# Expert slots of a product-key layer: weights from the exponentials of candidate sums, and 32 slots a head instead of 27

## The reference

```python
s0 = jnp.einsum('bshq,eq->bshe', _l2norm(q0), _l2norm(keys0))
s1 = jnp.einsum('bshq,eq->bshe', _l2norm(q1), _l2norm(keys1))
sc0, ix0 = jax.lax.top_k(s0, K)          # K = 16 of 64
sc1, ix1 = jax.lax.top_k(s1, K)
cs = (sc0[..., :, None] + sc1[..., None, :]).reshape(b, s, H, K * K)
ci = (ix0[..., :, None] + ix1[..., None, :]).reshape(b, s, H, K * K)
fs, pos = jax.lax.top_k(cs, K)           # 16 of the 256 pair sums
fi = jnp.take_along_axis(ci, pos, axis=-1)
w = jax.nn.softmax(fs, axis=-1)
inner = jnp.einsum('bsd,bshkd->bshk', hidden_states, expert_down[fi])
out = jnp.einsum('bshk,bshko->bso', gelu(inner) * w, expert_up[fi])
```

## Time and profile before

| | us |
|---|---|
| median of 3 runs | 446.78 (444.7 to 447.22) |
| span of the profiled execution, first to last instruction | 440.9 |
| mean granted TensorE clock | 0.714 of full speed |
| busy: TensorE, VectorE, ScalarE, GpSimd | 306.9, 350.6, 143.5, 190.4 |

### The profile page before, as it was taken

How to read it: one execution, slowest core, us unless ns; L and a number is a source line. 1 busy time by engine, 2 the same in 40 slices (tenths; PEclk the granted TensorE clock), 3 DMA queues, 4 the chain that set the end, 5 groups by cost and what they waited for, 6 DMA issues and landing times.

```text
span 440.9 us, 7832 instructions
## 1 busy us (share of the span) xinstructions
PE 306.9 (70%) x2271; PEld 224.6 (51%) x2271; DVE 350.6 (80%) x2183; ACT 143.5 (33%) x326; POOL 190.4 (43%) x391
## 2 busy tenths in 40 slices
PE   3168456784519587999795969998676569940496
PEld 1035234453307344698663547985443259820394
DVE  1957329238999998779999979999997799997941
ACT  2126231654414266451132464224040351021300
POOL 6319932326945384469352742203064302059000
PEclk9999567898655669586587886556668866585556
DMA  6000000000000000000000000000000000000000
GB/s 226 0 0 1 1 1 0 1 0 1 1 2 0 1 2 1 2 1 2 1 0 2 1 13 0 4 0 4 1 1 13 0 1 2 2 1 12 2 1 12
DMA packets 1634, 3.50 MB, mean 8 GB/s; under 512 B 180, under 2 KB 1205, under 8 KB 1592
## 3 DMA queue, kind: packets, MB, share of 16 engines
q1 hardware_dynamic: 1592, 3.01, 1.9%
HBM read 2.49 MB, written 0.52 MB: 7 GB/s over the span
## 4 chain that ended last, share of the span: by engine, by line
DVE 42%; PE 32%; ACT 11%; POOL 10%; issue 4%; DVEq 0%; ACTq 0%; POOLq 0%
PE bank L870 8%; PE bank L536 4%; DVE Sx L1356 4%; DVE i L1362 4%; DVE i L1363 4%; DVE segmax L1237 3%; DVE vraw L1359 3%; DVE vraw L1353 2%; ACT PT L1034 2%; POOL weights L1655 2%; PE bank L674 2%; PE bank L546 2%; PE bank L732 2%; POOL slots L1670 2%; PE bank L882 2%
## 5 line engine op out<-in xcount | busy, mean ns | idle before, releaser
L870 PE MATMUL bank<-weights,onehot 108*128 108x16 f16 x1024 | 68.6, 216 | 5.3 <-DVE onehot L493 5.3
L870 PEld LDWEIGHTS bank<-weights,onehot 108*128 108x128 f16 x1024 | 68.6, 174 | 6.5 <-DVE onehot L493 5.8
L1637 POOL TENSOR_TENSOR inv<-nrm,mhalf 128x16 f32<-128x16 f32 x8 | 23.4, 2923 | 40.4 <-DVE nrm L1369 40.4
L454 POOL TENSOR_TENSOR taps<-qpad,wa 128x128 f32<-128x128 f32 x96 | 36.1, 435 | 7.8 <-ACT qpad L923 7.7
L1550 POOL TENSOR_TENSOR rstd<-veps,mhalf 128x2 f32<-128x2 f32 x16 | 11.6, 726 | 41.0 <-DVE veps L1159 40.7
L1363 DVE FIND_INDEX8 i<-vraw,Sx 128x8 uint16<-128x64 f32 x128 | 28.1, 220 | 0.0
L1362 DVE FIND_INDEX8 i<-vraw,S 128x8 uint16<-128x64 f32 x128 | 28.1, 220 | 0.0
L536 PE MATMUL bank<-wa,hat 128*128 128x128 f32 x24 | 6.9, 382 | 30.0 <-ACT hat L908 29.9
L799 PE MATMUL bank<-KB,qsT 128*128 128x256 f32 x64 | 25.5, 568 | 0.9 <-ACT qsT L1066 0.9
L1356 DVE MATCH_REPLACE8 Sx<-vraw,S 128x64 f32<-128x64 f32 x128 | 25.2, 209 | 0.0
L1412 DVE MATCH_REPLACE8 cands<-c,cands 128x54 f32<-128x54 f32 x128 | 23.7, 199 | 0.0
(11 more groups left out here) (226 smaller groups left out, 785.1 us busy)
## 6 DMA issues: line engine op xcount, KB each, us to landing
wa<-wa_dram SPq DMA_DIRECT2D x1, 747.5 KB, 4.7
wb<-wb_dram SPq DMA_DIRECT2D x1, 707.0 KB, 5.4
x_sb<-x_dram SPq DMA_DIRECT2D x4, 128.0 KB, 3.8
out_dram<-eT SPq DMA_DIRECT2D x4, 128.0 KB, 1.7
onehot<-ws_dram SPq DMA_DIRECT2D x1, 448.0 KB, 6.0
bq_row<-rows_dram SPq DMA_DIRECT2D x1, 0.5 KB
onehot<-rows_dram SPq DMA_DIRECT2D x1, 13.5 KB
```

The source lines that it names most:

```text
L454: ins = eng.tensor_tensor(tv[:, :, :, ky, kx:kx + n], q, dw[:, ky, kx:kx + n].unsqueeze(1).unsqueeze(1).broadcast_to([P, G8, G8, n]), ALU. ...
L870: last = mm(o[:, g * 16:g * 16 + 16], OHv[:, c * NT + t, g], Rv[:, c, t, g, s], start=(c == 0 and s == 0), stop=(c == NCH - 1 and s == 1))
```

## The change

- Cell weights: ScalarE takes the exponential straight from the 54 candidate sums of a head (432 elements a partition and half) into `we`. The largest value is no longer subtracted: a sum of two cosines is at most 2, and the softmax divides it out. GpSimd's subtraction and its five products go; of `cells` the five expert sums stay. VectorE signals `cand_ready` behind its sums and waits for `exp_ready` before `chosen`. The marked candidates get a buffer of their own (`candm`), since the sums have to live until ScalarE has read them.
- Slots: there are 32 a head. The cells are numbered so that 32 of them can stay in place, and the other 22 are added to slots by four sums in place, in `wem`. The copies go. The slots fill 4 x 32 = 128 partitions, so all tiles and matmuls over slots have 128 rows.
- The weights are scaled from `wem` into `wn` as before, over 32 slots. The experts are copied out of `wem` by ScalarE into a new tile `es` (one instruction a half, in steps N2r and N2s of its list), and TensorE's slot transposes wait for it (`es_ready`) as well as for `wn`.
- ScalarE's N2p waits for TensorE's scatter of the image before, not for VectorE's read of its result.

```diff
-SLOT_SUMS = [
-    (1, 1, 1, 53, -1, 8),
...
-SLOT_COPIES = [(0, 0, 1, 1), (24, 17, 9, 2), (26, 32, 1, 1)]
-SLOTS = 27
+SLOT_SUMS = [(1, 8, 53, -1), (9, 4, 43, -3), (18, 4, 44, -3), (13, 2, 32, 4)]
+SLOTS = 32
...
-        A3a.2 F8c.1 A3b.2 A1b.2 N2q.0 A3c.2 F10a.1 F10b.1 F11t.1 A4.2 F11b.1 N3a.0 F5b.2 F12.1 F5c.2 N0a.1 N4.0
+        A3a.2 F8c.1 A3b.2 A1b.2 N2q.0 A3c.2 F10a.1 F10b.1 F11t.1 A4.2 F11b.1 N2r.0 N2s.0 N3a.0 F5b.2 F12.1 F5c.2 N0a.1 N4.0
...
-        candm = cand
+        candm = sb("candm", [NT * H, CELLS])
...
-        slots = sb("slots", [2, NT * H, SLOTS])
+        es = sb("es", [NT * H, SLOTS])
...
                 pe.wait_ge(slots_ready, NT * b + halves[-1] + 1)
-                for kind, src in (("w", wn[:, :, :]), ("e", slots[:, 1, :, :])):
+                pe.wait_ge(es_ready, NT * b + halves[-1] + 1)
+                for kind, src in (("w", wn[:, :, :]), ("e", es[:, :, :])):
...
-                ac.wait_ge(dv_ready, NT * b + t + 1)
-                fn(ab[:, h, :, :], dv[:, h, :, :], ACT.Exp).then_inc(ab_ready, 1)
+
+                ac.wait_ge(cand_ready, NT * b + t + 1)
+                fn(we[:, 0, h, :], cand[:, h, :], ACT.Exp).then_inc(exp_ready, 1)
...
             def N2p(b):
                 if b >= 1:
-                    read_out(ac, "G1", b - 1)
+                    full(ac, "G1", b - 1)
...
+            def expert_slots(b, t):
+                h = slice(t * H, t * H + H)
+                if b >= 1:
+                    full(ac, "eT", b - 1)
+                ac.wait_ge(merged_ready, NT * b + t + 1)
+                fn(es[:, h, :], wem[:, 1, h, 0:SLOTS], ACT.Copy).then_inc(es_ready, 1)
...
-                link(last)
+                last.then_inc(cand_ready, 1)
+                dve.wait_ge(cand_ready, NT * b + t + 1)
...
+                dve.wait_ge(exp_ready, NT * b + t + 1)
                 dve.wait_ge(we_ready, NT * b + t + 1)
...
-                src, dst = wem[:, :, h, :], slots[:, :, h, :]
-                for at, c, step, n in SLOT_COPIES:
-                    g_.tensor_copy(dst[:, :, :, at:at + n], src[:, :, :, c:c + step * (n - 1) + 1:step])
-                for at, c, step, c2, step2, n in SLOT_SUMS:
-                    end = c2 + step2 * (n - 1) - 1
-                    last = g_.tensor_tensor(dst[:, :, :, at:at + n], src[:, :, :, c:c + n],
-                                            src[:, :, :, c2:end:step2], ALU.add)
-                link(last)
-                g_.tensor_tensor(wn[:, h, :], slots[:, 0, h, :],
+                for at, n, c, step in SLOT_SUMS:
+                    end = c + step * (n - 1) + (1 if step > 0 else -1)
+                    last = g_.tensor_tensor(wem[:, :, h, at:at + n], wem[:, :, h, at:at + n],
+                                            wem[:, :, h, c:end:step], ALU.add)
+                last.then_inc(merged_ready, 1)
+                pool.wait_ge(merged_ready, NT * b + t + 1)
+                g_.tensor_tensor(wn[:, h, :], wem[:, 0, h, 0:SLOTS],
```

43 lines of the change are left out of this document (18 added, 25 removed).

## The result

The changed kernel takes **442.08 us** in the median (439.24 to 443.43, 12 runs), the kernel before, run beside it, 446.26 us (442.84 to 450.35, 12 runs). The ratio is **0.9926, with a 95% interval of 0.9899 to 0.9954**: 0.7% faster, some 3.3 us. (The two medians lie 4.2 us apart, since the times of each kernel come in steps of about 2 us; the ratio is the better measure.) The prediction was 445.0 us, with a range of 442.0 to 448.4. By the prediction's own bound of 0.5% the kernel is faster.

What follows compares the result with a forecast made beforehand. VectorE was taken as the bound, busy 350.6 of 440.9 us. Terms -0.42 -0.28 -0.42 +1.69 -0.42 -1.95 = -1.80 us gave 439.1, plus 5.9 around the span 445.0 us; range 442.0 to 448.4, the forecast's own 443.6 to 446.6.

Steps and rivals of the forecast that it cites:

- the prediction's own bound of 0.5%: Whole kernel: 0.5% (2.2 us) taken as the measurement's own width; faster means below 444.55 us.
- The time around the span: Whole kernel: 5.9 us around the profiled span of 440.9, from the runs' median of 446.78, added to 439.1.
- The sums: VectorE's candidate sums: 0.42 us gained each at 134, 244 and 328 us, 0.42 lost at the last image.
- Merges and `kBD`, image 0: Image 0: shorter merge lets `kBD` start with `khT`; 0.7 us gained, of which 0.42 is counted in the sums.
- The clock at 174 us: Rival: image 2's stretch at 174 us gets the upper clock, 4.4 us less, 440.6 us; chance 0.10.
- the stretch: TensorE from `fT` to the first-attention outputs (L631): 9.64 us in image 2, 5.2 us in image 3 before the change.
- The wait for `es`, image 1: Image 1: `es` copies stand behind sixteen exponentials on ScalarE, so VectorE waits longer for eT; 1.69 us lost.
- The other rival, the clock against the change: Stretch behind image 1's slot transposes (from 261 us) falls to the lower clock: 4.4 us more, 449.4 us; chance 0.10.
- Image 2: Image 2's merge: TensorE reaches the transposes at 340.38 anyway, out of its fillers; nothing gained, nothing lost.
- The tail: Image 3: merge and eT come before VectorE is free, so its wait of 2.37 us goes; 1.95 us gained.
- The rival that had this gain eaten: Last image: cells hold VectorE or eT is late, so the 1.95 us is gone; 446.9 us, chance 0.12.
- the one on rows: Rival: 128 instead of 108 rows cost 3.2 us in the tail's scatter; 448.2 us, chance 0.05.

Runs made afterwards that it cites:

- the second profile of after: The changed kernel, unchanged, run once more beside the kernel before: ratio 0.9921 to before, median 441.59 us.
- esg: The changed kernel with the es copies moved from ScalarE to GpSimd, behind wn of each half: ratio 0.9933 to the kernel before, median 442.14 us.
- hold: The changed kernel, only that GpSimd's cells wait for the candidate sums of their half: ratio 0.9913 to the kernel before, median 441.37 us.
- weights_only: The kernel before with only the changed weights (exponential of the sums, expert cells only); 27 slots merged as before: ratio 0.9945 to before, 443.31 us.
- merges_only: The changed kernel with weights made as before (subtraction, exponential of 256 elements, products), so only the slots changed: ratio 0.9922 to before, 441.66 us.
- the second profile of before: The kernel before, unchanged, profiled a second time (444.5 us); against itself its ratio is 0.9991, median 446.29 us.

## Why the prediction came out as it did

**The time around the span.** The prediction added 5.9 us to the profiled span, from a median of runs and one execution. In every run whose span and time are both known the difference is about 1.8 us (446.35 and 444.5; 443.43 and 441.6). The other 4.1 us are, all but 0.5, that one execution's quicker start (3.6). For the forecast it made no difference: a sum on top of a median is right whatever the profile's luck. But the profile before was not the median execution, and comparing it with a profile of after would have shown a change of 0.7 us for the worse.

**The sums.** Right at image 0's first half: 0.88 us. The cells beside image 0's second half made it 1.52, where 1.30 was kept. In image 1 it was 0.88 in the second profile of after and 1.66 in the first. There VectorE had come 0.95 us late to the segment maxima, by the lower clock at 224 us, and the cells fell on the sums: so the 0.42 was gained in one execution and 0.36 lost in the other. In image 2 it was 1.23 and 0.88, 0.07 and 0.42 gained: the prediction had no overlap there, though by its own numbers `if_` (329.29) came before the end of the sums (329.4). In the last image 0.22 and 0.33 were lost where 0.42 was taken. What was missed: at 142 us the gain is 0.79 and 0.61 in the two profiles and not 0.42. 0.20 of it is there because the products that GpSimd no longer makes ran beside other VectorE work too. `centBD` behind the searches, a product of two operands, goes from 0.49 to 0.29 us:

```profile
139.26 0.49 DVE L1216 TENSOR_TENSOR centBD<-cent,wb 128x128 f32<-128x128 f32 x1
```

```profile
142.82 0.29 DVE L1223 TENSOR_TENSOR centBD<-cent,wb 128x128 f32<-128x128 f32 x1
```

**Merges and `kBD`, image 0.** Forecast 0.42 + 0.28 = 0.70 us; the table has 0.82 and 0.92 at negM. The merges take 1.32 + 0.62 us with a gap of 0.08, together 2.0 where 1.96 was worked out. `kBD` starts as soon as `khT` is there:

```profile
167.13 1.05 POOL L1612 TENSOR_TENSOR kBD<-khT,wa 128x512 f32<-128x512 f32 x1 [1.63 <-ACT khT L950]
```

**The clock at 174 us.** It was a rival with a chance of 0.10 and a gain of 4.4 us. It is what happened: fully, at 1.00, in five of the eleven profiles that have any part of the change, and for the larger part of the stretch, at 0.76, in the other six. The step that failed is the one that read the level in one profile as given. The price failed as well: 4.4 us was TensorE's saving (4.2 as measured), and VectorE gets 2.4 or less, because `xln` on GpSimd is late next.

**The wait for `es`, image 1.** Forecast 1.69 us lost. From 246.1 to 260.1 after loses 1.44 and 1.56, the wait itself goes from 1.13 to 2.76 and 2.68: mechanism, place and size are right. (The working has 259.05 for a sum of 259.09, and nothing hangs on it.) The sum was right to count it, and yet it was not worth its removal: esg took 2.07 us off the wait and ended where after did. The other rival, the clock against the change, came true in the experiments, in the stretch that it named: from 260 to 274 esg loses 2.75 us, hold 1.68 and weights_only 1.67; seven of the twelve profiles of the changed and the edited kernels have the stretch at 0.6 to 0.7. But it was not more idle time ahead that brought it: in esg TensorE waited 2.08 and 1.67 us there, in the two profiles of after 4.78 and 3.88, and these had 2.4 GHz.

**Image 2.** Forecast 0 for the merge; measured 0.93 and 1.41 us less of waiting for eT. This is the term of the sum that was mis-sized. It was argued that TensorE gets to the slot transposes out of its fillers anyway. In before that is so, but at 1.2 GHz: the two fillers ahead take 1.06 us. In all profiles of merges_only, weights_only and after they take 0.59 to 0.65, and then it matters that `wn` had come only 0.12 us before (340.26 against 340.38). With the short merge it is there in time; with the long one, in weights_only, TensorE waits for it:

```profile
341.88 1.10 PE L534 MATMUL bank<-wa,wn 128*108 128x128 f32 x4 [0.45 <-POOL wn L1668]
```

The transposes follow the clock too. In merges_only (the rows below) and the second profile of after both groups take 0.60 us instead of 1.06; in the first profile of after they take 0.88 and 1.06, and the gain is the smaller 0.93. So the term needs the shorter merge and the upper clock together, and the prediction took neither as a gain here.

```profile
340.71 0.60 PE L530 MATMUL bank<-wa,wn 128*128 128x128 f32 x4
341.14 0.60 PE L530 MATMUL bank<-wa,es 128*128 128x128 f32 x4
```

**The tail.** Forecast 2.37 us of wait gone, less 0.42 for the sums: 1.95. From 357 us on (-1.29 and -2.52, between two columns of the table) to the second eT at 415 (-3.24 and -4.37) the two profiles of after gain 1.95 and 1.85. The wait is gone as said and the sums lose 0.22 and 0.33; what nothing in the prediction had are 0.38 us lost between the first and the second eT. VectorE's products for `R` now run beside the second merge and take 2.14 us instead of 1.70.

```profile
409.58 2.14 DVE L1482 TENSOR_TENSOR weights<-W,cands 128x256 f16<-128x256 f16 x8
```

The rival that had this gain eaten is excluded, and so is the one on rows.

**Together**: leave out the stretch (2.42) and the late maxima behind it (0.96), and the steps of the sum come to 3.42 - 2.42 + 0.96 = 1.96 us in the profile of after, against a forecast of 1.80. That it is so close is luck: image 2's eT gave 0.9 us more than forecast, and the sums took 0.8 more in image 1 and 0.35 in image 2. In the second profile of after the same reckoning (0.97 for the stretch, nothing lost at the maxima) leaves 3.8. So the forecast was right in direction, in the wait for `es` and in the tail; it was too small by image 2 and by the clock, whose better level it held to be improbable. How much of the 3.3 us is the clock's stays open: what it gives at 174 us it partly takes at 224, and in no run was it held at one level.

## What to carry to other kernels

Compare two profiles only from a point behind which they differ by the change alone: set both to zero at the last place that the change can't have touched. One execution's luck of the clock (3.6 us here) is otherwise larger than the effect.

A wait that two edits remove is gained once, and a gain in mid-kernel is only worth what is left of it at the end: the twelve profiles of the changed and the edited kernels all came to 246 us between 1.7 and 3.7 us early, and all but one left 274 us with 1.03 us or less. The gain that reached the end in each of the eleven that have any part of the change is that of the last image.

Where a second engine's small operations fall beside those of the bounding one, it is worth trying one wait to keep them apart: hold took 0.64 us off one group of sums by an added wait on an idle engine, and the searches behind did not suffer. A gain of the whole kernel by it is not shown.

## What the runs showed of the hardware

The same kernel has more than one time. The matmuls at 42.15 us take 1.94 us in one execution of the kernel before and 3.60 in the other, and with what follows up to 78 us the total differs by 3.6 us. The runs of the unchanged kernel show this as steps, near 442.7, 444.7 and 446.4 us, and those of after near 439.3, 441.3 and 443.2. In ten of the fourteen profiles the record of the clock covers this place, and it tells the two starts apart. Below are 17 matmuls at 1.00 in merges_only and 9 at 0.50 in the second profile of after (length, busy, count, clock, DMA share, GB/s of TensorE alone).

```profile
42.15:44.00 1.85, 1.85 (x17) 1.00 0.00 0
```

```profile
42.15:44.00 1.85, 1.85 (x9) 0.50 0.00 0
```

So the slow start is the lower clock. In the second profile of before the same view shows 1.00 beside 9 matmuls, but there (as in the first of after) the record begins only behind 66 us, and a view has 1.00 where there is no record. Ahead of the first record the durations have to be read: sixteen outputs take 1.94 us at the upper level here and 3.60 at the lower. Further on, as at 174 us, clock and durations go together.

Behind the start the level can be the same from one execution to the next, as in the two profiles of before (9.64 us at 0.54 twice for the stretch of image 2), or not, as in the two of after (5.47 us at 1.00 and 7.08 at 0.76). Idle time of TensorE 9 us ahead, from 0 to 0.5 us, does not go with it; the moment at which the clock had last risen does, and the runs leave open whether that is the cause.

VectorE's two-operand tensor operations slow down beside GpSimd's (0.88 to 1.66 us, 0.29 to 0.49, 1.70 to 2.14), MAX8 does not (1.02 to 1.03 with and without). Scatter pairs with 108 and 128 rows take the same 66.7 ns, at 1.2 GHz.
